# First attention layer: row maxima one and a half batches ahead, output rows in the big ring, epsilon on GpSimd

## The reference

```python
x = x + L0_xattn(layernorm(x), ctx, ctx)
x = x + L0_ffn(layernorm(x), ...)          # 8 experts, the two best of each token
x = x + L1_xattn(ctx, layernorm(x), ...)
x = x + L1_ffn(layernorm(x), ...)

def L0_xattn(Q, K, V):                     # 16 heads of 16 columns, no weights
    scores = einsum('bhqd,bhkd->bhqk', q, k) * 0.25
    return einsum('bhqk,bhkd->bhqd', softmax(scores), v)
```

## Time and profile before

| | us |
|---|---|
| median of 3 runs | 1277.8 |
| lowest, highest | 1277.34, 1283.1 |
| profiled execution, its own time | 1278.05 |
| its span in the trace | 1276.3 |
| first reduction of the first layer starts at | 18.7 |
| last one starts at | 252.1 |

### The profile page before, as it was taken

The page is one execution under the profiler, slowest core; times in us unless marked ns, Lnnn a source line. Parts: engine busy times, 40 slices in busy tenths (PEclk is TensorE's granted clock), DMA queues, the critical chain, the costliest instruction groups (busy, mean ns, idle before and its releaser), DMA issues. The chain is left out here.

```text
span 1276.3 us, 26854 instructions
## 1 busy us (share of the span) xinstructions
PE 1140.6 (89%) x9615; PEld 932.8 (73%) x9616; DVE 934.5 (73%) x1378; ACT 739.0 (58%) x978; POOL 585.2 (46%) x555
## 2 busy tenths in 40 slices
PE   3788999978879999999999999925898999999997
PEld 2455666548879999999999999814666666668886
DVE  7798999728548887887878877568788888843332
ACT  3376777766445665565455556233777777774443
POOL 1367776444458588653202000067777776201221
PEclk9999999998989999999999999956999999999999
DMA  5556766428963645563113111055566665411221
GB/s 189 191 192 200 242 209 236 146 92 281 344 218 119 203 148 172 170 201 107 41 49 107 41 49 41 26 200 171 195 217 214 204 201 194 165 44 44 79 73 45
DMA packets 120983, 193.41 MB, mean 152 GB/s; under 512 B 12160, under 2 KB 64384, under 8 KB 120768
## 3 DMA queue, kind: packets, MB, share of 16 engines
q1 hardware_dynamic: 95840, 140.71, 32.5%
q0 software_dynamic: 12576, 39.07, 9.9%
q10 hardware_dynamic: 12480, 12.47, 2.9%
HBM read 91.80 MB, written 49.55 MB: 111 GB/s over the span
## 5 line engine op out<-in xcount | busy, mean ns | idle before, releaser
L2128 PE MATMUL y_ps<-e_w,hiddenT_hi 128*128 x624 | 225.2, 404 | 1.6 <-DVE slot_y L2232 1.6
L2164 ACT ACTIVATE hidden<-hidden 128x1024 f32<-128x1024 f32 x78 | 82.8, 1062 | 186.2 <-DVE hidden L2197 186.2
L2111 PE MATMUL h_ps<-slot_xT_hi,tile_w_hi 128*128 128x256 f32 x624 | 178.1, 285 | 3.0 <-DVE slot_xT_lo L2215 3.0
L1458 DVE TENSOR_REDUCE neg_max<-big 128x4 fp32r<-128x1024 f32 x128 | 155.3, 1221 | 31.5 <-PE big L1215 29.8
L2111 PE MATMUL h_ps<-slot_xT_lo,tile_w_hi 128*128 128x256 f32 x624 | 177.8, 285 | 0.0
L2111 PE MATMUL h_ps<-slot_xT_hi,tile_w_lo 128*128 128x256 f32 x624 | 177.7, 285 | 0.0
L2129 PE MATMUL y_ps<-e_w,hiddenT_lo 128*128 x624 | 175.3, 281 | 0.0
L603 DVE TENSOR_REDUCE neg_max<-big 128x4 fp32r<-128x1024 f32 x128 | 155.2, 1222 | 21.2 <-PE big L404 18.8
L535 ACT ACTIVATE probs<-big 128x1024 f32<-128x1024 f32 x128 | 131.0, 1023 | 57.7 <-PE big L415 56.8
L1374 ACT ACTIVATE probs<-big 128x1024 f32<-128x1024 f32 x128 | 131.0, 1026 | 45.0 <-PE big L1226 44.8
L2221 DVE TENSOR_TENSOR hiddenT_lo<-hidden,hiddenT_hi 128x1024 fp32r<-128x1024 f32 x78 | 101.5, 1342 | 58.2 <-ACT hiddenT_hi L2175 58.2
(11 more groups left out here) (238 smaller groups left out, 2600.3 us busy)
## 6 DMA issues: line engine op xcount, KB each, us to landing
k_stack<-k_cut SPq DMA_DIRECT2D x96, 256.0 KB, 3.9
q_stack<-q_cut SPq DMA_DIRECT2D x96, 256.0 KB, 3.0
e_w<-in_L_ffn_w POOLq DMA_DIRECT2D x10, 1024.0 KB, 5.9
slots_out<-slot_y ACTq DMA_DIRECT2D x39, 256.0 KB, 2.2
slots_in<-staging POOLq DMA_DIRECT2D x38, 256.0 KB, 2.7
slot_x<-slots_in SPq DMA_DIRECT2D x38, 256.0 KB, 2.8
vals<-in_v_wide SPq DMA_DIRECT2D x16, 512.0 KB, 4.1
v_wide<-v_out SPq DMA_DIRECT2D x16, 512.0 KB, 5.8
```

The lines of the kernel that those rows point to most:

```text
L1458: nc.vector.tensor_reduce(neg_max[m % 2][:, :, :, g].rearrange("p q a -> p a q").bitcast(F32R), big[bank][:], AX.X, ALU.max, negate=True). ...
L2111: last = nc.tensor.matmul(h_ps[k][:, f % HF, :], w1[w][b.u][:, c, f * P:(f + 1) * P], xT[a][b.u][:, c, :], start=(n == 0), stop=(n == 3 * ...
L2128: nc.tensor.matmul(y_ps[q][:].rearrange("p s d -> p (s d)"), hT[0][o.u][:, f, rows], both, start=(f == 0), stop=False)
```

## The change

The maxima in slot g of body b are now those of number (b + 1) x 8 + g + 4, counted over all batches: one and a half batches ahead. What feeds the maxima (q, k, x statistics) is moved by half a body with them. Output rows are one use of the big ring, after the score of slot 2, in eight transposes, and VectorE empties them with one reciprocal and one multiplication in slot 3. Logits come a body later, in slot 1. The negative rows are turned in slot 4 instead of slot 0. GpSimd adds epsilon, takes the residual ahead of the first power, and SyncE's order is another. The number of bodies grows by one.

```diff
-    FIRST, END = -5, BATCHES + 2
+    FIRST, END = -5, BATCHES + 3
-    LN_STEPS = 2 * QT + 1
+    LN_STEPS = 2 * QT
+    OUT_AT = 2
+    HALF = PAIRS // 2
+
+    def maxima(b, g):
+
+        return divmod((b + 1) * PAIRS + g + HALF, PAIRS)
+
     spare_order, big_order = [], []
     for b in range(FIRST, END):
         spare_order += [(name, t) for name, t in (
-            (("pv", 3), b - 1), ("negT", b + 1), ("qT", b + 3), (("out", 0), b - 1), (("out", 1), b - 1), (("pv", 0), b),
-            ("normT", b - 2), (("pv", 1), b), ("logits", b - 2), (("pv", 2), b)) if has(t)]
+            (("pv", 3), b - 1), ("logits", b - 3), (("pv", 0), b), ("negT", b + 1), ("normT", b - 2), (("pv", 1), b),
+            ("qT", b + 3), (("pv", 2), b)) if has(t)]
         for g in range(PAIRS):
-            big_order += [(name, t) for name, t in ((("max", g), b + 2), (("score", g), b)) if has(t)]
+            m, gm = maxima(b, g)
+            big_order += [(name, t) for name, t in ((("max", gm), m), (("score", g), b), ("out" if g == OUT_AT else None, b - 1))
+                          if has(t) and name]
...
             def body(b):
+                if has(b - 2):
+                    sp.wait_ge(norm2_ready, (b - 1) * QT)
+                    sp.dma_start(tiled(dram["norm2"], b - 2), norm2[b % 2][:]).then_inc(norm2_stored[b % 2], 16)
+                if has(b + 2):
+                    load_v(b + 2)
                 if has(b + 5):
                     load_x(b + 5)
                 if has(b + 4):
                     load_k(b + 4)
-                if has(b - 2):
-                    sp.wait_ge(norm2_ready, (b - 1) * QT)
-                    sp.dma_start(tiled(dram["norm2"], b - 2), norm2[b % 2][:]).then_inc(norm2_stored[b % 2], 16)
+                if has(b + 1):
+                    stack_neg(b + 1)
                 if has(b + 3):
                     stack_k(b + 3)
-                if has(b + 2):
-                    load_v(b + 2)
-                if has(b + 1):
-                    stack_neg(b + 1)
                 if has(b + 3):
                     stack_q(b + 3)
...
-            def power(veps, rs, ln_done, rs_ready, t):
+            def power(mv, veps, rs, ln_done, rs_ready, t):
                 pool.wait_ge(ln_done, (t + 1) * LN_STEPS)
+                nc.gpsimd.tensor_scalar(veps[:], mv[:, :, 1], EPS, None, ALU.add).then_inc(rs_ready, 1)
+                pool.wait_ge(rs_ready, 2 * t + 1)
                 nc.gpsimd.tensor_tensor(rs[:], veps[:], neg_half[:, 0:QT], ALU.pow).then_inc(rs_ready, 1)
 
...
+                read_big(pool, ("out", d))
                 for q in range(QT):
-                    read_spare(pool, (("out", q), d))
...
                 if has(b + 3) and b + 3 >= RAMP:
                     split_k(b + 3)
+                if has(b - 1):
+                    residual(b - 1)
                 if has(b + 4):
-                    power(var_eps, rstd, ln_step, rstd_ready, b + 4)
+                    power(mean_var, var_eps, rstd, ln_step, rstd_ready, b + 4)
                 if has(b + 4) and b + 4 >= RAMP:
...
                 if has(b - 1):
-                    residual(b - 1)
                     if has(b - 3):
                         pool.wait_ge(norm2_stored[(b - 1) % 2], (b - 1) // 2 * 16)
                         full_spare(pool, ("normT", b - 3))
-                    power(var_epsb, rstdb, ln2_step, rstd2_ready, b - 1)
+                    power(mean_varb, var_epsb, rstdb, ln2_step, rstd2_ready, b - 1)
...
-            def out_rows(d, q):
+            def out_rows(d):
                 for gg in range(GROUPS):
                     read_spare(pe, (("pv", gg), d))
-                bank = free_spare(pe, (("out", q), d))
-                for gg in range(GROUPS):
-                    last = nc.tensor.transpose(spare[bank][:, gg * P:(gg + 1) * P], outT[d % 2][:, gg, q * P:(q + 1) * P], ident[:])
-                last.then_inc(filled[bank], 1)
+                bank = free_big(pe, ("out", d))
+                for q in range(QT):
+                    for gg in range(GROUPS):
+                        last = nc.tensor.transpose(big[bank][:, q, gg // 2, gg % 2 * P:(gg % 2 + 1) * P], outT[d % 2][:, gg, q * P:(q + 1) * P], ident[:])
+                last.then_inc(big_filled[bank], 1)
...
             def body(b):
                 for g in range(PAIRS):
-                    if has(b + 2):
-                        row_max(b + 2, g)
+                    m, gm = maxima(b, g)
+                    if has(m):
+                        row_max(m, gm)
                     if has(b):
                         score(b, g)
                     if g == 0:
                         if has(b - 1):
                             pv(b - 1, 3)
-                        if has(b + 1):
-                            turn_neg(b + 1)
                     elif g == 1:
-                        if has(b + 3):
-                            turn_q(b + 3)
+                        if has(b - 3):
+                            logits(b - 3)
+                    elif g == OUT_AT:
                         if has(b - 1):
-                            out_rows(b - 1, 0)
-                    elif g == 2:
-                        if has(b - 1):
-                            out_rows(b - 1, 1)
+                            out_rows(b - 1)
                     elif g == 3:
                         if has(b):
                             pv(b, 0)
                     elif g == 4:
+                        if has(b + 1):
+                            turn_neg(b + 1)
                         if has(b - 2):
                             turn_norm2(b - 2)
                     elif g == 5:
                         if has(b):
                             pv(b, 1)
                     elif g == 6:
-                        if has(b - 2):
-                            logits(b - 2)
+                        if has(b + 3):
+                            turn_q(b + 3)
                     elif g == 7:
                         if has(b):
                             pv(b, 2)
...
                 if has(b - 2):
-                    full_spare(act, (("out", 1), b - 2))
+                    full_big(act, ("out", b - 2))
...
             def body(b):
-                if has(b + 4) and b + 4 < 4:
-                    clear_k(b + 4)
-                if has(b + 3) and b + 3 < RAMP:
-                    k_hi_out(b + 3)
...
                 for g in range(PAIRS):
+                    if g == HALF and has(b + 4) and b + 4 < 4:
+                        clear_k(b + 4)
+                    if g == HALF and has(b + 3) and b + 3 < RAMP:
+                        k_hi_out(b + 3)
                     if has(b):
                         exp(b, g)
                     if g == 0:
                         if has(b - 1):
                             pv_out(b - 1, 3)
+                    elif g == 4:
                         if has(b + 1):
                             neg_out(b + 1)
-                    elif g == 1:
+                        if has(b - 2):
+                            norm2_out(b - 2)
+                    elif g == 6:
                         if has(b + 3):
                             q_hi_out(b + 3)
-                    elif g == 4:
-                        if has(b - 2):
-                            norm2_out(b - 2)
                     elif g in (3, 5, 7):
                         if has(b):
                             pv_out(b, (g - 3) // 2)
...
                 dve.wait_ge(step, t * LN_STEPS + QT)
                 alone(dve)
                 for q in range(QT):
                     nc.vector.bn_aggr(mv[:, q, :], s6[:, q, :]).then_inc(step, 1)
-                dve.wait_ge(step, t * LN_STEPS + 2 * QT)
-                nc.vector.tensor_scalar(veps[:], mv[:, :, 1], EPS, None, ALU.add).then_inc(step, 1)
...
-            def out_rows(d, q):
-                bank = full_spare(dve, (("out", q), d))
-                heads = spare[bank][:].rearrange("p (h r) -> p h r", r=VW)
-                nc.vector.reciprocal(recip[:, q, :], heads[:, :, DH]).then_inc(recip_done, 1)
-                dve.wait_ge(recip_done, d * QT + q + 1)
+            def out_rows(d):
+                bank = full_big(dve, ("out", d))
+                heads = big[bank][:].rearrange("p a q s -> p (a q s)").rearrange("p (q h r) -> p q h r", q=QT, r=VW)
+                nc.vector.reciprocal(recip[:], heads[:, :, :, DH]).then_inc(recip_done, 1)
+                dve.wait_ge(recip_done, d + 1)
                 if has(d - 2):
                     dve.wait_ge(y_ready, (d - 1) * QT)
-                nc.vector.tensor_tensor(att[d % 2][:, q, :].rearrange("p (h d) -> p h d", d=DH), heads[:, :, 0:DH],
-                                        recip[:, q, :].unsqueeze(2).to_broadcast([P, HEADS, DH]), ALU.mult).then_inc(freed[bank], 1)
+                nc.vector.tensor_tensor(att[d % 2][:].rearrange("p q (h d) -> p q h d", d=DH), heads[:, :, :, 0:DH],
```

(46 more changed lines are left out.)

6 lines of the change are left out of this document (3 added, 3 removed).

## The result

The changed kernel takes 1301.4 us at the median of its four runs (1298.2, 1298.8, 1303.9, 1313.6) where the kernel before takes 1277.8: a ratio of 1.019, 95% interval 1.016 to 1.022. It is slower, by more than the 16.7 forecast, and inside the range. In a second series on one chip, six runs of the changed kernel have a median of 1301.0 beside 1281.75 for 23 of the kernel before: 1.0135, interval 1.0101 to 1.0169, or 19.3 us.

The account below looks back on a forecast made before the run. Neither VectorE nor TensorE alone was taken to bound the kernel: a slot costs its longer side. The terms 16.9 - 3.4 + 4.0 - 2.0 + 1.0 = +16.5 took 1278.05 to 1294.6, forecast 1294.5, range 1274 to 1314.

Parts of the forecast that it names:

- The closed line: First attention layer, one batch's chain from M4 to the next M4: 15.7 against 14.4, +1.3 a batch, +16.9 over batches 1 to 13.
- M4: TensorE's row maxima of slot 4, said to wait about 1.1 for VectorE's output multiplication; M, S and R number by slot.
- R4: VectorE's reduction of the maxima M4, forecast 0.54 after them.
- VectorE's saving worth nothing: First layer: fewer epsilons, reciprocals and multiplications, worth 0.7 a batch only where VectorE is the longer side.
- Rival A: First layer: VectorE's saving counts in full, 0.74 in each of 14 batches, time 1262; chance 0.13.
- The w2T load: Issued at about M4 + 9, it lands late and delays batch 12: +4.0 in all, between nothing and 6.
- The stall that goes: One old batch of 16.40, with output rows queued behind q in the spare banks, loses its stall: -2.0.
- Lead and tail: First layer's ends: shorter lead of maxima -3.4 (start alone -5.6); exposed chain after the last scores +1.0, 0.3 to 1.5.
- The rest of the program: Stages after the first layer start at its end and move with it, with no term of their own.
- a sign of being wrong: The prediction is wrong if, among other signs, time is saved or lost outside the first 300 us.
- rival C: TensorE, idle about 1.1 before M4, falls to 1.2 GHz: 1.5 each in half of the batches, 1306; chance 0.07.
- Rival D: Negative rows, turned in slot 4, come late for S0; a microsecond more costs 1 a batch, 1309; chance 0.05.

Follow-up runs that it names:

- e0_after: The changed kernel run again with nothing altered, for its own spread: 1301.0 us at the median.
- e5: The kernel before with only the output rows moved to the big ring, emptied in slot 3: 1296.9 us, ratio 1.0105.
- e1: The changed kernel with VectorE emptying the output rows in slot 2 instead of slot 3: 1282.3 us, ratio 0.9995 to the kernel before.
- e10: The changed kernel with VectorE's output multiplication done three times, the first two read by nobody: 1335.1 us.
- e11: The changed kernel with the output multiplication done three times and fourteen useless transposes on TensorE in the gap: 1318.3 us.
- e6: The kernel before with the epsilon added by GpSimd instead of VectorE: 1280.7 us against 1281.3, ratio 1.0000.
- e7: The changed kernel with output rows emptied in slot 2, w2T halves issued earlier and the extras spread over slots: 1268.7 us, ratio 0.9910 to the kernel before.
- e2: The changed kernel with the two w2T halves issued right behind the stacking of the negative rows: 1292.7 us.
- e9_before: The kernel before run again with nothing altered, for a second profile: 1278.3 us.
- e4: The changed kernel with its output rows back in the two spare banks, the rest of the change kept: 1302.8 us, ratio 1.0156.

## Why the prediction was right, and where it was off

*The closed line.* Right, nearly step by step. From M4 of one batch (140.07 in e0_after) to M4 of the next (155.77):

| step | predicted | measured |
|---|---|---|
| M4 to R4 | 0.54 | 0.61 |
| R4 to R5 | 1.83 | 1.80 |
| R5 to R6 | 2.10 | 1.91 |
| R6 to R7 | 2.2 | 2.21 |
| R7 to S0 | 1.26 | 1.34 |
| S0 and product | 1.44 | 1.43 |
| M1, S1, logits | 1.66 | 1.66 |
| M2, S2, output rows | 1.87 | 1.83 |
| M3 to R3 | 0.54 | 0.55 |
| R3 to M4 | 2.28 | 2.36 |
| sum | 15.7 | 15.70 |

(S0 is the score of the next body's slot 0, O the output rows' transposes.) e5 shows that the big ring's placing alone makes the line, e1 that emptying one slot earlier opens it, e10 and e11 that every added microsecond counts in full.

*VectorE's saving worth nothing.* Right: e6 measured 0 for the epsilons, and the merged multiplication stands in the line itself. Rival A (faster) is out for this order. Whether its premise holds in another order is open: e7 is faster than the kernel before, but evens out the slots as well. By the Trainium skill (Perfetto Trace Analysis, Identifying the Most-Contended Engine; the prediction names the section behind it) the engine with the highest occupancy is to be relieved first; here that engine was relieved by 0.8 a batch and the batch grew by 1.3.

*The w2T load.* Right in mechanism and nearly in size. It was issued at M4 + 9.0, as worked out, landed in 3.84 instead of 4.45, and held ScalarE 5.2. Batch 12 took 21.21, 5.5 over its neighbours, where the kernel before paid 1.5: +4.0. By the medians, taking it away is worth 8.3 (e2), twice the term, of which the profiles show 5.1.

*The stall that goes.* Mis-sized: forecast −2.0. The kernel before has a batch of 16.6 and one of 15.6 in both of its profiles' first layers (16.58 and 15.67; 16.59 and 15.64), 3.4 over 14.4 together. I had counted one, and read the stall and TensorE's fall as one thing. They are two: in e9_before TensorE stands 1.47 at the same place and does not fall, and a stand of 0.98 further on is followed by a fall:

```profile
108.91 0.63 PE L454 MATMUL spare<-ident,outT 128*128 128x128 f32 x4 [1.47 <-DVE q_cut L634]
...
110.67 1.07 PE L428 MATMUL spare<-probs,vals 128*32 128x256 f32 x16 [0.21 <-DVE att L644]
...
181.45 0.63 PE L454 MATMUL spare<-ident,outT 128*128 128x128 f32 x4 [0.98 <-DVE q_cut L634]
...
183.20 1.94 PE L428 MATMUL spare<-probs,vals 128*32 128x256 f32 x16 [0.21 <-DVE att L644]
```

*Lead and tail.* The first score goes at 37.10 in e0_after, where it went at 42.47: -5.4, forecast -5.6. The tail is +1.0 as forecast (from the last output multiplication to the last logits 9.96 before, 10.97 in e0_after). The whole layer ends 12.8 later than in the first profile of before and 16.8 later than in the second (the rank subtraction at 303.1, 290.3 and 286.3). My sum of +16.5 was made against the first, so it is 3.7 too high. Most of that lies in the first profile's ramp, which I had not looked at for falls: it has three products of 1.93 (49.81, 54.52 and 59.23), the second profile has one (49.70), and the first output rows are done at 69.44 there and at 66.37 in the second, 3.1 sooner. Against the second profile, which doesn't have them, the sum is 0.3 too low.

*The rest of the program.* I said that later stages move with this one. They do, but with their own spread: spans 1276.3, 1275.9 and 1297.4 are 21 apart, of which the first layer is 12.8 or 16.8. The rest is 4 in the rank stretch against the first profile, a spread that e9 shows without the change, and 4.2 to 4.4 behind the experts' first product, most of it in the second layer (from its first reduction to its last 260.9, before 258.6) and the last stage. The second layer's part is spread too: the first profile of the changed kernel has 258.6 there. For the last stage, 1.3 longer in both profiles of the changed kernel (122.7, before 121.4), I found no wait that the change would explain, but the variant e4 takes 121.1 there; that part stays open. So 8.3 of the 21 were lost behind the first layer, which I had named as a sign of being wrong, and that the total came out within 5 us of the sum owes something to luck: against the same profile the layer's +12.8 is under it, and the rest, which I had put at nothing, is over it.

*The step that was off* is rival C's price and chance. I had a fall in half of the batches at 1.5 each, for 0.07. It costs 1.37 a batch, and it came behind eleven waits of one execution, in five batches of e5's, in one of e0_after's. The forecast of 1294.5 (0.2 over the median plus my sum, which is 1294.3) is an execution without falls, and the fastest of ten was 1295.5. The 6.9 between it and the median of the first series is more than I can assign: partly falls in some batches, partly the spread of later stages. What the row had told me was that a fall is possible after such a gap; the right reading would have been a chance in each execution, not a rival for all of them. What decides in one execution no run shows.

*Rival D, the negative rows late,* did not show: TensorE's first score of a batch waits for the reduction R7 (0.34 before it at 147.94 in e0_after), not for the rows.

## What to carry to other kernels

Before moving work off the busiest engine, follow the ring: a bank that one engine fills and another empties behind its next operation on the same ring closes a line, and every part of that line counts in full while the engines idle around it. The cure can be one slot in one engine's order (18.7 us here), and while the line is closed, saved instructions beside it do not count. A load at the end of a queue moves with whatever is issued ahead of it, so look it up there when a stack is shifted by some slots. Look at TensorE's idle places in a loop: a stand is not always followed by a fall, but two kernels that differ only in useless transposes in one of 2.62 were 16.8 us apart, in favour of the one that does more.

## What the runs showed that I had not expected

- The same code with the same wait of 1.17 had TensorE fall to 1.2 GHz behind eleven waits of one execution (17.06 a batch) and behind the first alone in another (15.69 in the batches after); e5 changed between the two inside one loop (17.05, then 15.76). A time of a kernel with such a gap is a mixture.
- A lead can vanish with the same code: a first layer that ended 4.0 sooner (e9_before against before) gave nearly all of it back in the rank stretch, where the experts' first product is at 360.5 and 360.7. 2.8 of it went in two places where TensorE, after a stand, ran slow in one profile and not in the other, 1.0 in VectorE's additions.
- In the kernel before, a stand of 1.47 passed without a fall and one of 0.98 was followed by one, in the same execution (e9_before).
- With a gap of 2.62 (e10) nine batches in a row alternate between a long fall and a shorter one, 19.40 and 18.16.
